# Weighing of values split by queries into two halves, one behind each maximum block

## The chip, the core and the metric

One Trainium2 chip, one of its cores. The metric is the device time of one execution in microseconds (us), as the median of several runs. Everything is one program on one core: TensorE (PE in the profile), VectorE (DVE), ScalarE (ACT), GpSimd (POOL) and the queue of SyncE (SP), each with its own list of instructions, ordered against each other by semaphores.

## What is computed

A block of three layers over x of shape (2, 1024, 128) in float32: half a mixture-of-experts feed-forward, self-attention, half the same feed-forward again. The change touches the attention alone:

```python
qkv = x @ W_qkv_v.T @ W_qkv_u.T            # 16 heads of 8
scores = einsum('bhtd,bhsd->bhts', q, k) / sqrt(8)
attn = softmax(scores)                     # over 1024 keys
y = einsum('bhts,bhsd->bhtd', attn, v)
```

## The kernel before

Attention is cut into 16 **units** (`UNITS`): four heads (`GH`) by 512 queries (`QW`). A unit has eight **chunks** (`CHUNKS`) of 128 keys. A softmax needs the maximum over all keys of a query first, so a unit has two kinds of scores:

- **Maximum blocks** (16 for a unit, `MBLOCKS`): `max_scores(j, part)`, line 1170, writes scores of 128 queries by 512 keys; two parts fill the two banks of `pair[j % 2]`. VectorE's `row_max(j)`, line 914, then takes the maximum of the 1024 columns. With two pairs of banks, TensorE may write block j once block j - 2 is read (`smax_read`). The maxima go through GpSimd (lines 501 to 505), a transpose on TensorE (`m_transpose`, line 1205), a copy on ScalarE (`m_out`, line 659) and a DMA into three more rows of the stack `q_stack`, so that later scores come with the maximum already subtracted. The blocks run ahead: beside chunk c of unit u stand blocks `16(u + 1) + 8 + 2c` and the next one (`blocks_beside`). From chunk 4 of unit 14 on there are none left.
- **Scores of a chunk** (four, one for each head): `scores(u, c, k)`, line 1182, 128 keys by 512 queries, into a ring of three banks (4, 5, 7). ScalarE takes the exponential of each (line 674) into `prob`. The k-th score of the ring can start when ScalarE has read the bank three users back. The transposes of `m_transpose` and `o_transpose` take a turn in the same ring (`bank_users`).

Both kinds use only half of the array's rows: heads 0 and 1 lie in partitions 0 to 63 of the stacks, heads 2 and 3 in 64 to 127. `HEAD_OF_STEP` makes steps 0 and 1 of a chunk heads 2 and 3 (upper half), steps 2 and 3 heads 0 and 1 (lower half). The first block beside a chunk is of a head in the lower half, the second of one in the upper half. Two matmuls on different halves run at the same time.

- **Weighing**: `weigh(u, c)`, line 1191, four float32 matmuls, one for each head, with the values (128 keys by 32 columns) as weights and the exponentials (128 by 512) streamed. The four heads take the four groups of 32 columns of the array and run side by side, in two passes each. They add up over the chunks in bank 6. The weighing waits for all four exponentials of its chunk (`prob_ready`), and the first one of a unit for the copy of bank 6 (`sums_out`, line 691, `oT_ready`). At the end it gives `pv_done`, on which ScalarE waits before it overwrites `prob` two chunks later.

TensorE's order within chunk c, by hand: first block part 0, score 0, first block part 1, score 1, score 2, weighing of chunk c - 1, transposes if any, second block part 0, score 3, second block part 1. In units 14 and 15 some chunks end with work for what follows attention (`beside`: transposes at lines 1216 and 977, projections at line 1225). In chunk 2 TensorE transposes the sums of the unit before (`o_transpose`, line 1199) and VectorE divides by the softmax's denominators (`store_norm`, lines 921 and 924), there between the two maxima of the chunk.

Of the kernel before, what the change touches and what calls it, by code (L numbers as in the profile page):

```python
# [35 lines left out]
GH = 4  # L36
GROUPS = 2 * HEADS // GH
UNITS = 2 * GROUPS
CHUNKS = SEQ // P
QW = 512  # L40
STEPS = CHUNKS * GH
AHEAD = 8
# [28 lines left out]
def bank_users():  # L71

    users = [("m", 0)]
    for u in range(UNITS):
        for c in range(CHUNKS):
            users += [("score", STEPS * u + GH * c + k) for k in range(GH - 1)]
            if c == O_CHUNK and u:
                users.append(("o", u - 1))
            if c == M_CHUNK and u + 1 < UNITS:
                users.append(("m", u + 1))  # L80
            users.append(("score", STEPS * u + GH * c + GH - 1))
    return users + [("o", UNITS - 1)]
# [25 lines left out]
def at_least(eng, sem, value):  # L108

    if not isinstance(value, int) or value > 0:  # L110
        eng.wait_ge(sem, value)


def build(nc, x_in, w_qkv_v, w_qkv_ut, w_o_v, w_o_ut, gate_w, sh_gate, sh_up, sh_down, r_gate, r_up, r_down, out):
# [3 lines left out]
    with ExitStack() as ctx:  # L118
# [426 lines left out]
        def _(act):  # L545
# [64 lines left out]
            def attention():  # L610
# [55 lines left out]
                def unit(u):  # L666

                    turns_left = UNITS - u
                    for c in range(CHUNKS):
                        for k in range(GH):  # L670
# [4 lines left out]
                                                 scale=SCALE).then_inc(prob_ready, 1)  # L675
                            if i == 2 and u:
                                sums_out(u - 1)
                            if i == GH * M_CHUNK + 2 and turns_left > 1:
                                m_out(u + 1)
# [29 lines left out]
        def _(dve):  # L709
# [181 lines left out]
            def attention():  # L891
# [35 lines left out]
                def unit(u):  # L927

                    for c in range(CHUNKS):
                        blocks = blocks_beside(u, c)  # L930
                        for j in blocks[0:1]:
                            row_max(j)
                        if c == O_CHUNK and 0 < u < UNITS - 1:
                            store_norm(u - 1)
                        for j in blocks[1:2]:
                            row_max(j)

# [28 lines left out]
        def _(pe):  # L966
# [146 lines left out]
            def attention():  # L1113
# [70 lines left out]

                def weigh(u, c):

                    pe.wait_ge(prob_ready, STEPS * u + GH * (c + 1))
                    if c == 0:
                        at_least(pe, oT_ready, u)
                    for h in range(GH):  # L1190
                        ins = nc.tensor.matmul(bank[6][32 * h:32 * (h + 1), :], v_grp[u // 2 % 2][:, c, h, :], prob[c % 2 * GH + h],  # L1191
                                               start=(c == 0), stop=(c == CHUNKS - 1))
                    ins.then_inc(pv_done, 1)

# [44 lines left out]
                def unit(u):  # L1239
# [5 lines left out]
                    for c in range(CHUNKS):  # L1245
                        blocks = blocks_beside(u, c)
                        for part in range(2):
                            for j in blocks[0:1]:
                                max_scores(j, part)
                            scores(u, c, part)  # L1250
                        scores(u, c, 2)
                        if c:
                            weigh(u, c - 1)
                        elif u:
                            weigh(u - 1, CHUNKS - 1)
                        if c == O_CHUNK and u:
                            o_transpose(u - 1)
                        if c == M_CHUNK and u + 1 < UNITS:
                            m_transpose(u + 1)
                        for j in blocks[1:2]:  # L1260
                            max_scores(j, 0)
                        scores(u, c, 3)
                        for j in blocks[1:2]:
                            max_scores(j, 1)
                        for work, quad_done in beside.get((UNITS - u, c), ()):
# [14 lines left out]
                for u in range(UNITS):  # L1280
                    unit(u)
                weigh(UNITS - 1, CHUNKS - 1)
                logits(1, 0)
# [35 lines left out]
```

## Time and profile before

| | |
|---|---|
| median of 3 runs | 673.07 us (672.56 to 674.61) |
| the profiled execution | 678.38 us, its span 676.6 us |
| feed-forward, then projections and the stacks | 0 to about 179 us of the span |
| maxima of unit 0 and half of unit 1 | about 180 to 210 us |
| units 0 to 15 | about 210 to 540 us |
| second feed-forward | about 540 to 676.6 us |
| TensorE, VectorE, ScalarE, GpSimd busy | 573.9, 454.8, 376.0, 144.0 us |

The times in the rows are microseconds from the start of the span. A row of the timeline joins neighbouring instructions of the same kind and gives the start of the first, the time until the last one ends, and how many there are. A matmul's duration holds its way through the array, so consecutive ones overlap; what one costs in a row of them is the distance from start to start.

### The profile page before, as it was taken

To read this page: it belongs to the slowest core of one execution; us is meant where nothing else is said; L and a number is where in the kernel's file an instruction comes from. 1 tells how busy PE (TensorE), PEld (TensorE's weight loads), DVE (VectorE), ACT (ScalarE), POOL (GpSimd) and SP (SyncE) were. 2 spreads that over 40 slices of the span, in tenths; PEclk is the share of its full clock that TensorE was granted. 3 is DMA by queue.
4 is the path that set the end of the run, shared out by engine and by line. 5 is a ranking of instruction groups with operands and counts; after the bars stand their busy time and mean duration, and the time that the engine had idled before them with its cause. 6 is when DMAs were issued, how large, how long until landed. Compare 5 with 4: busy or idle time off the path is not lost.

```text
span 676.6 us, 11663 instructions
## 1 busy us (share of the span) xinstructions
PE 573.9 (85%) x3560; PEld 206.0 (30%) x3560; DVE 454.8 (67%) x815; ACT 376.0 (56%) x816; POOL 144.0 (21%) x228
## 2 busy tenths in 40 slices
PE   2984999824589999999999999999999968589991
PEld 2643445412121122222222222222223444434440
DVE  6542334347378999999999999999992557124442
ACT  2211344313404988888988888888888821023340
POOL 2471245513500000000000000000000004414442
PEclk9988999957755999999999999999999969879996
DMA  9995223123321000101000010000000000111114
GB/s 231 325 342 161 82 83 85 44 64 108 141 77 48 2 2 3 47 1 43 8 15 35 1 49 2 2 1 3 1 2 2 1 0 29 46 31 56 50 40 134
DMA packets 52295, 40.56 MB, mean 60 GB/s; under 512 B 4905, under 2 KB 49598, under 8 KB 52240
## 3 DMA queue, kind: packets, MB, share of 16 engines
q1 hardware_dynamic: 49168, 35.58, 17.8%
q0 software_dynamic: 3072, 4.28, 2.0%
q8 instruction: 30, 0.49, 0.3%
q14 instruction: 25, 0.20, 0.1%
HBM read 26.85 MB, written 14.88 MB: 62 GB/s over the span
## 4 chain that ended last, share of the span: by engine, by line
PE 53%; DVE 16%; issue 10%; DMA 8%; ACT 6%; SPq 2%; another core or an unknown queue 2%; POOL 2%; POOLq 0%; DVEq 0%; ACTq 0%
PE bank L1191 13%; PE pair L1170 12%; DVE rowmax L914 9%; PE pair L1061 7%; PE bank L1182 5%; PE bank L1078 4%; ACT arena L674 4%; DMA xe<-rows 3%; PE pair L1070 3%; PE pair L985 2%; POOL rows L467 1%; PE bank L1049 1%; PE bank L1199 1%; PE pair L977 1%
## 5 line engine op out<-in xcount | busy, mean ns | idle before, releaser
L914 DVE TENSOR_REDUCE rowmax<-pair 128x1 f32<-128x1024 f32 x256 | 301.7, 1219 | 29.2 <-PE pair L1170 24.4
L674 ACT ACTIVATE arena<-bank 128x512 f32<-128x512 f32 x512 | 271.5, 605 | 48.9 <-PE bank L1182 43.6
L1182 PE MATMUL bank<-q_stack,k_stack 51*128 51x512 bf16 x512 | 164.9, 388 | 4.1 <-ACT arena L674 1.2
L1170 PE MATMUL pair<-k_stack,q_stack 48*128 48x512 bf16 x512 | 153.6, 407 | 15.0 <-DMA k_stack<-k_parts 5.2
L1191 PE MATMUL bank<-arena 128*32 128x512 f32 x1024 | 137.5, 609 | 0.2 <-ACT arena L674 0.2
L474 POOL DMA_INDIRECT y<-yb,slot_token x64 | 62.9, 982 | 100.0 <-ACT yb L587 82.3
L864 DVE TENSOR_TENSOR arena<-pair,arena 128x256 f32<-128x256 f32 x64 | 27.2, 424 | 82.2 <-ACT arena L582 65.4
L1170 PEld LDWEIGHTS pair<-k_stack,q_stack 48*128 48x128 bf16 x512 | 29.6, 95 | 155.4 <-DVE rowmax L914 130.8
L1061 PE MATMUL pair<-w_exp,xeT 128*64 x128 | 69.1, 623 | 0.4 <-ACT xeT L577 0.4
L1063 PE MATMUL pair<-w_exp,xeT 128*64 128x512 f32 x128 | 69.2, 623 | 0.0
L1182 PEld LDWEIGHTS bank<-q_stack,k_stack 51*128 51x128 bf16 x512 | 39.2, 94 | 66.8 <-ACT arena L674 56.2
L501 POOL TENSOR_TENSOR mpart<-zeros,rowmax 128x16 bf16<-128x16 f32 x16 | 3.5, 222 | 248.1 <-DVE rowmax L914 248.1
L587 ACT ACTIVATE yb<-bank 128x128 f32<-128x128 f32 x64 | 17.8, 277 | 54.1 <-PE bank L1080 48.3
L467 POOL DMA_INDIRECT rows<-xn,slot_i x32 | 31.2, 974 | 74.0 <-DVE slot_i L836 65.1
L977 PE MATMUL pair<-identf,xn 128*128 128x128 f32 x48 | 11.3, 392 | 40.7 <-DVE xn L746 40.3
L1078 PE MATMUL bank<-w_exp,arena 128*64 x256 | 41.6, 285 | 0.2
L1080 PE MATMUL bank<-w_exp,arena 128*64 128x128 f32 x256 | 41.6, 286 | 0.0
L582 ACT ACTIVATE arena<-pair 128x256 f32<-128x256 f32 x64 | 24.6, 385 | 28.3 <-PE pair L1063 27.4
L1015 PE MATMUL bank<-w_sh,arena 128*128 128x128 f32 x128 | 19.0, 311 | 13.9 <-DVE xres L806 12.4
L1191 PEld LDWEIGHTS bank<-arena 128*32 128x32 f32 x1024 | 20.2, 108 | 32.0 <-issue 30.9
L1078 PEld LDWEIGHTS bank<-w_exp,arena 128*64 128x64 f32 x256 | 26.2, 136 | 9.9 <-issue 6.1
L1070 PE MATMUL pair<-identf,arena 128*128 128x128 f32 x128 | 28.0, 300 | 0.0
(135 smaller groups left out, 534.2 us busy)
## 6 DMA issues: line engine op xcount, KB each, us to landing
xe<-rows SPq DMA_DIRECT2D x64, 66.0 KB
w_exp<-in_r_gate SPq DMA_DIRECT2D x4, 1024.0 KB
w_exp<-in_r_up SPq DMA_DIRECT2D x4, 1024.0 KB
w_exp<-in_r_down SPq DMA_DIRECT2D x8, 512.0 KB
rows<-empty_row SPq DMA_DIRECT2D x1, 2112.0 KB, 11.6
rows<-empty_row SPq DMA_DIRECT2D x32, 66.0 KB
xnT<-y SPq DMA_DIRECT2D x8, 256.0 KB, 3.5
q_parts<-arena SPq DMA_DIRECT2D x12, 128.0 KB, 2.6
```

The source lines that it names most:

```text
L467: nc.gpsimd.indirect_dma_start(rows_dram[n], bass.IndirectOffsetOnAxis(slot_i[:, t:t + 1].bitcast(U32), 0), xn[:, t, :], None).then_inc(sc ...
L474: nc.gpsimd.indirect_dma_start(y_dram[n], bass.IndirectOffsetOnAxis(slot_token[:, r:r + 1].bitcast(U32), 0), yb[r % 4][:, :], None, bounds ...
L674: nc.scalar.activation(prob[c % 2 * GH + HEAD_OF_STEP[k]], ring_bank("score", STEPS * u + i), ACT.Exp, scale=SCALE).then_inc(prob_ready, 1)
L914: nc.vector.tensor_reduce(rowmax[u % 2][:, m:m + 1], pair[j % 2][:, :], AX_X, ALU.max).then_inc(smax_read, 1)
L1061: nc.tensor.matmul(bank[r % 2][0:PAGE, :], xeT[r % 2][:, 0:PAGE], w_exp[:, bass.ds(e, 2 * INNER)], start=True, stop=True)
L1063: nc.tensor.matmul(bank[r % 2][PAGE:P, :], xeT[r % 2][:, PAGE:P], w_exp[:, j * WROW:j * WROW + 2 * INNER], start=True, stop=True).then_inc ...
L1070: ins = nc.tensor.transpose(bank[2 + r % 2][:, c * P:(c + 1) * P], h_sb[r % 2][:, c * P:(c + 1) * P], identf[:, :])
L1078: nc.tensor.matmul(bank[(4, 7)[r % 2]][0:PAGE, 0:P], hT_sb[r % 2][:, c * P:c * P + PAGE], w_exp[:, bass.ds(e + at, P)], start=(c == 0), st ...
L1080: ins = nc.tensor.matmul(bank[(4, 7)[r % 2]][PAGE:P, 0:P], hT_sb[r % 2][:, c * P + PAGE:(c + 1) * P], w_exp[:, j * WROW + at:j * WROW + at ...
L1170: ins = nc.tensor.matmul(pair[j % 2][:, part * BANK:(part + 1) * BANK], q_stack[r][rows, half, l, t * P:(t + 1) * P], k_stack[r][rows, l, ...
L1182: nc.tensor.matmul(ring_bank("score", i), k_stack[r][rows, l, c * P:(c + 1) * P], q_stack[r][rows, half, l, :], start=True, stop=True).the ...
L1191: ins = nc.tensor.matmul(bank[6][32 * h:32 * (h + 1), :], v_grp[u // 2 % 2][:, c, h, :], prob[c % 2 * GH + h], start=(c == 0), stop=(c == ...
```

## The change

The weighing is cut by queries into two halves of 256 columns (`PARTS`, `WEIGHED`): `weigh(u, c, w)`. TensorE's order in a chunk becomes: first block part 0, score 0, first block part 1, score 1, weighing's first half, second block part 0, score 2, second block part 1, score 3, weighing's second half, then transposes and the work beside. In chunk 1 both halves stand at the end, since bank 6 is still being copied out. VectorE takes both maxima of a chunk before it divides (`store_norm`). ScalarE's `sums_out` and `m_out` move behind the fourth exponential of their chunk, and the ring's turns for the transposes behind the fourth score. Scores, blocks, exponentials and their number stay.

```diff
+PARTS = 2
+WEIGHED = QW // PARTS
@@ bank_users
-            users += [("score", STEPS * u + GH * c + k) for k in range(GH - 1)]
+            users += [("score", STEPS * u + GH * c + k) for k in range(GH)]
             if c == O_CHUNK and u:
                 users.append(("o", u - 1))
             if c == M_CHUNK and u + 1 < UNITS:
                 users.append(("m", u + 1))
-            users.append(("score", STEPS * u + GH * c + GH - 1))
@@ ScalarE, unit
-                            if i == 2 and u:
+                            if i == 3 and u:
                                 sums_out(u - 1)
-                            if i == GH * M_CHUNK + 2 and turns_left > 1:
+                            if i == GH * M_CHUNK + 3 and turns_left > 1:
                                 m_out(u + 1)
@@ VectorE, unit
-                        for j in blocks[0:1]:
+                        for j in blocks:
                             row_max(j)
                         if c == O_CHUNK and 0 < u < UNITS - 1:
                             store_norm(u - 1)
-                        for j in blocks[1:2]:
-                            row_max(j)
@@ TensorE, weigh
-                def weigh(u, c):
+                def weigh(u, c, w):
 
-                    pe.wait_ge(prob_ready, STEPS * u + GH * (c + 1))
-                    if c == 0:
-                        at_least(pe, oT_ready, u)
+                    cols = slice(w * WEIGHED, (w + 1) * WEIGHED)
+                    if w == 0:
+                        pe.wait_ge(prob_ready, STEPS * u + GH * (c + 1))
+                        if c == 0:
+                            at_least(pe, oT_ready, u)
                     for h in range(GH):
-                        ins = nc.tensor.matmul(bank[6][32 * h:32 * (h + 1), :], v_grp[u // 2 % 2][:, c, h, :], prob[c % 2 * GH + h],
-                                               start=(c == 0), stop=(c == CHUNKS - 1))
-                    ins.then_inc(pv_done, 1)
+                        ins = nc.tensor.matmul(bank[6][32 * h:32 * (h + 1), cols], v_grp[u // 2 % 2][:, c, h, :],
+                                               prob[c % 2 * GH + h][:, cols], start=(c == 0 and w == 0),
+                                               stop=(c == CHUNKS - 1 and w == PARTS - 1))
+                    if w == PARTS - 1:
+                        ins.then_inc(pv_done, 1)
@@ TensorE, unit
-                        for part in range(2):
-                            for j in blocks[0:1]:
-                                max_scores(j, part)
-                            scores(u, c, part)
-                        scores(u, c, 2)
-                        if c:
-                            weigh(u, c - 1)
-                        elif u:
-                            weigh(u - 1, CHUNKS - 1)
+                        weighed = (u, c - 1) if c else (u - 1, CHUNKS - 1)
+                        for w in range(PARTS):
+                            for part in range(2):
+                                for j in blocks[w:w + 1]:
+                                    max_scores(j, part)
+                                scores(u, c, 2 * w + part)
+                            if c != 1 and weighed[0] >= 0:
+                                weigh(*weighed, w)
+                        if c == 1:
+                            for w in range(PARTS):
+                                weigh(*weighed, w)
                         if c == O_CHUNK and u:
                             o_transpose(u - 1)
                         if c == M_CHUNK and u + 1 < UNITS:
                             m_transpose(u + 1)
-                        for j in blocks[1:2]:
-                            max_scores(j, 0)
-                        scores(u, c, 3)
-                        for j in blocks[1:2]:
-                            max_scores(j, 1)
@@ TensorE, after the units
-                weigh(UNITS - 1, CHUNKS - 1)
+                for w in range(PARTS):
+                    weigh(UNITS - 1, CHUNKS - 1, w)
```

## Rows read from the trace of the kernel before

**Rows 1.** The page's first part: busy time, share of the span, instructions.
```profile
PE 573.9 (85%) x3560; PEld 206.0 (30%) x3560; DVE 454.8 (67%) x815; ACT 376.0 (56%) x816; POOL 144.0 (21%) x228
```

**Rows 2.** Groups of instructions, 240 to 500: busy us, mean ns; idle us before, by releaser.
```profile
L914 DVE TENSOR_REDUCE rowmax<-pair 128x1 f32<-128x1024 f32 x206 | 242.6, 1219 | 10.1 <-PE pair L1170 5.8
L674 ACT ACTIVATE arena<-bank 128x512 f32<-128x512 f32 x412 | 218.5, 605 | 33.9 <-PE bank L1182 29.0
```

**Rows 3.** Waits, 240 to 500: who for whom, total us, times, longest us.
```profile
PEld pair L1170 <- DVE rowmax L914: 96.9, 148, 0.8
```

**Rows 4.** Timeline of VectorE: start, us until last end; ends of 13 units, then one.
```profile
240.23 7.16 DVE L914 TENSOR_REDUCE rowmax<-pair 128x1 f32<-128x1024 f32 x6
...
358.89 2.36 DVE L914 TENSOR_REDUCE rowmax<-pair 128x1 f32<-128x1024 f32 x2 [0.26 <-PE pair L1170]
...
361.87 7.16 DVE L914 TENSOR_REDUCE rowmax<-pair 128x1 f32<-128x1024 f32 x6
...
503.76 3.62 DVE L914 TENSOR_REDUCE rowmax<-pair 128x1 f32<-128x1024 f32 x3
```

**Rows 5.** The same timeline asked for stretches that hold two neighbouring maxima each.
```profile
352.53 2.48 DVE L914 TENSOR_REDUCE rowmax<-pair 128x1 f32<-128x1024 f32 x2
353.80 2.35 DVE L914 TENSOR_REDUCE rowmax<-pair 128x1 f32<-128x1024 f32 x2
354.94 2.56 DVE L914 TENSOR_REDUCE rowmax<-pair 128x1 f32<-128x1024 f32 x2
```

**Rows 6.** Timeline of TensorE in short stretches, one chunk of unit 7.
```profile
353.16 0.39 PE L1182 MATMUL bank<-q_stack,k_stack 51*128 51x512 bf16 x1
...
353.89 0.37 PE L1170 MATMUL pair<-k_stack,q_stack 48*128 48x512 bf16 x1
354.11 0.37 PE L1170 MATMUL pair<-k_stack,q_stack 48*128 48x512 bf16 x1
354.32 0.38 PE L1182 MATMUL bank<-q_stack,k_stack 51*128 51x512 bf16 x1
354.63 0.64 PE L1191 MATMUL bank<-arena 128*32 128x512 f32 x4
355.08 0.61 PE L1191 MATMUL bank<-arena 128*32 128x512 f32 x4
355.63 0.39 PE L1170 MATMUL pair<-k_stack,q_stack 48*128 48x512 bf16 x1
```

**Rows 7.** Timeline, the weight loads (PEld) of that weighing.
```profile
354.63 0.16 PEld L1191 LDWEIGHTS bank<-arena 128*32 128x32 f32 x8 [0.30 <-issue]
```

**Rows 8.** Timeline of ScalarE: after the score of 353.16, and four exponentials on end.
```profile
353.59 2.31 ACT L674 ACTIVATE arena<-bank 128x512 f32<-128x512 f32 x4 [0.17 <-PE bank L1182]
...
522.40 2.06 ACT L674 ACTIVATE arena<-bank 128x512 f32<-128x512 f32 x4 [0.32 <-PE bank L1182]
```

**Rows 9.** Timeline of TensorE: transposes of the sums, the block behind them.
```profile
340.33 0.65 PE L1199 MATMUL bank<-identf,oT 128*128 128x128 f32 x4
...
340.92 0.39 PE L1170 MATMUL pair<-k_stack,q_stack 48*128 48x512 bf16 x1
```

**Rows 10.** Timeline of VectorE in chunks 1 and 2 of unit 0.
```profile
217.25 2.35 DVE L914 TENSOR_REDUCE rowmax<-pair 128x1 f32<-128x1024 f32 x2 [2.03 <-PE pair L1170]
219.91 7.23 DVE L914 TENSOR_REDUCE rowmax<-pair 128x1 f32<-128x1024 f32 x6 [0.30 <-PE pair L1170]
```

**Rows 11.** The stretch 216 to 218: busy us of the engines, TensorE's granted clock.
```profile
216.00:218.00 2.00, 2.00 (x12) 0.53 (x8) 0.75 (x1) 0.92 (x2) 0.00 (x0) 0.50 0.12 49
```

**Rows 12.** Timeline of TensorE in unit 15, where no blocks are left.
```profile
520.98 1.07 PE L1191 MATMUL bank<-arena 128*32 128x512 f32 x8
...
523.05 0.39 PE L1182 MATMUL bank<-q_stack,k_stack 51*128 51x512 bf16 x1 [0.47 <-ACT arena L674]
...
531.72 1.07 PE L1191 MATMUL bank<-arena 128*32 128x512 f32 x8
...
534.15 1.06 PE L1191 MATMUL bank<-arena 128*32 128x512 f32 x8
```

## The prediction

> **What bounds the kernel now.** I read the page first: TensorE is busy for 85% of the span, VectorE for 67%, ScalarE for 56% [rows 1]. That mixes stages, so the groups of instructions for 240 to 500 us come next, the stretch of whole attention units. There VectorE's maxima alone are busy for 242.6 of 260 us and ScalarE's exponentials for 218.5 [rows 2]; and in the waits TensorE stands 96.9 us waiting for a maximum to free its banks, in 148 places [rows 3]. It looks as if VectorE were the bound, with 10.1 us of idle time left to win [rows 2]. That reading is too coarse, and the timeline of VectorE shows why. One unit takes (503.76 - 240.23) / 13 = 20.27 us [rows 4]. Neighbouring maxima start at 352.53, 353.80 and 354.94 us [rows 5]: the steps are 1.27, 1.14 and, since the pair from 354.94 lasts 2.56 us against 1.22 us for one, 1.34 us. A maximum is shown busy for 1.22 us but can follow the one before by 1.14, because the two overlap; so a step of 1.27 is a wait of 0.13 that no idle column shows. Every second step is short (1.14: the data had been there), every other one is 1.26 to 1.48 and more at chunk 2. VectorE's floor for a chunk is 2 x 1.142 = 2.284 us; the chunks take 2.40 to 2.56.
>
> What it waits for is a **loop through TensorE**, read from one chunk [rows 6]. The maximum that starts at 352.53 ends at 353.75 and frees its pair; 0.11 us later (353.86, a plain release elsewhere takes 0.05) come first block part 0 (353.89), part 1 with score 1 beside it (354.11), score 2 (354.32), the weighing (354.63), second block part 0 (355.63) and, 0.22 later, part 1 (355.85), whose result is there 0.38 us later; the next maximum of that pair of banks starts at 356.27. From the end of a maximum to there it is 2.46 to 2.52 us, in which nothing waits but for a little at score 2 (its bank). The second block is late because the whole weighing, 1.00 us, stands ahead of it. Two maxima end to end (1.142 + 1.214 = 2.356) and this path (2.46) make two chunks: (2.356 + 2.46) / 2 = 2.41 us for one, which is what is seen. Whatever else stands in that path (o_transpose 0.59 us [rows 9], m_transpose, one matmul, so at most a step of 0.22, score 2 waiting behind the copy of the sums) is added in full: hence gaps like the 0.26 us [rows 4]. So neither TensorE's throughput nor VectorE's bounds it, but the order between them.
>
> **The change, part by part.**
>
> *TensorE's own work for a chunk.* Start to start [rows 6]: block to block with a score beside it 0.22; last score to weighing 0.31; first to second pass of the weighing 0.45; second pass to the next block 0.55. Before: four such steps of 0.22 (parts of both blocks; scores 0, 1, 3 ride beside them), 0.31 and 1.00: 2.19 us. After: each half of a chunk has 0.226 + 0.306 and half a weighing. A pass streams 512 columns in 0.427 (0.45 less what the first loads cost, 0.026); with half the columns it is 0.213, so a half weighing takes 0.24 + 0.33 = 0.57, and half a chunk 0.226 + 0.306 + 0.57 = 1.10, the chunk 2.20. The cut costs 0.14 of streaming overhead and one more change of shape (0.09), and wins the 0.22 in which score 2 had no block beside it: nothing in sum. The eight weight loads of a weighing now meet passes half as long; they are through in 0.16 us [rows 7], which is under 0.213, so I cost them at nothing; uncovered they would be 0.16 for each half (below). Bound of the half weighing from both sides: 0.50 (exactly half) and 1.00 (no shorter at all); I take 0.57, since the pass's length follows the columns in the transposes too: four of 128 float32 columns take 0.65 us in all [rows 9].
>
> A rule of the Trainium skill speaks against the change here: TensorEngine Tiling (Array Packing), Tiling Modes, says that changing the tiling mode drains the engine. The row agrees in kind: 0.31 instead of 0.22 into the weighing, and about 0.1 out of it, 0.2 for a round trip. With two round trips instead of one the page's rule makes the chunk 0.2 us longer on TensorE, and that is in the 2.20 above.
>
> *The path to the blocks.* A release, 0.05 to 0.12; part 0, part 1 0.226; result and start of the maximum 0.41: 0.70 to 0.76 us after the maximum of that pair has ended. The other pair's maximum gives 1.142 - 0.07 = 1.07 us of cover. So VectorE finds every block ready as long as TensorE comes less than 0.3 to 0.37 us after the release; by its own work (1.10 for half a chunk against VectorE's 1.142) it comes 0.04 early. VectorE becomes the bound: 2.284 us for a chunk.
>
> *Where a wait is new.* The first half now stands behind score 1 and waits for all exponentials of the chunk before; behind it on TensorE are second block and scores 2 and 3, on which VectorE and ScalarE wait. Score to exponential 0.43 (353.16 to 353.59), exponentials on end (2.06 - 0.60) / 3 = 0.48 apart [rows 8]. From the start of score 2: exponential 2 at 0.43, exponential 3 at 0.90, its end 1.50, seen at 1.56; TensorE is there at 1.142 + 0.53 = 1.67. It fits by 0.11. The turns of the ring's three banks have more room. ScalarE's load is 4 x 0.48 = 1.93 for a chunk: below the bound.
>
> *Chunks with extra work.* Chunk 1 has no half weighing in the middle and both at its end, four passes on end, about 1.00: its next block is 0.39 after its release, against 0.37 of cover: 0.02 lost. Chunk 2: transposes 0.59 [rows 9] at its end; VectorE divides after both maxima, 0.62 us from the end of a maximum to the next (361.25 to 361.87 [rows 4]). The transposes are through about 0.2 before VectorE asks for them, and the division gives TensorE the time for them. Score 2 of chunk 3 waits for the division (ring) about when it comes up anyway. m_transpose, under 0.22, goes into the cover. The copy of the sums moves one exponential later; the weighings that wait for it are at chunk 1's end. The moved DMA of m (its issue follows ScalarE's copy) has three chunks to land. So a unit is 16 x 1.142 + 0.62 + 0.02 = 18.9 us, by TensorE's own count 8 x 2.20 + 0.59 + 0.2 - 0.2 = 18.2, hidden. **Gain 20.27 - 18.9 = 1.35 a unit**, for the 13 units of [rows 4] and the one from 219.91 to 240.23: 14 x 1.35 = -18.9 us.
>
> *Beginning.* In unit 0 the clock is at 0.50 (1.2 GHz) until about 218 [rows 11], and VectorE idles 2.03 and 0.30 us behind a cold weighing of 1.9 us [rows 10]. With second block ahead of it the idle comes in two smaller pieces; I get the maximum of 219.91 at about 219.1: -0.8, and +0.5 at worst if the clock rises later.
>
> *End.* Without blocks (from chunk 4 of unit 14) the cut only costs: the scores 1 and 2 and the scores 3 and 0 no longer stand next to each other on different halves. A plain chunk is 2.39 now (weighing at 520.98; last score before the next at 523.05, plus 0.31) with 0.47 of waiting for ScalarE [rows 12]; after, TensorE alone needs 2 x (0.215 + 0.317 + 0.57) = 2.20: -0.2, in four chunks. A chunk with transposes beside it is 2.43 (531.72 to 534.15 [rows 12]), no waiting; after 2.20 + 0.59 = 2.79: +0.35, in about seven with such work, projections too. In sum +1.6.
>
> Sum: -18.9 - 0.8 + 1.6 = -18.1. The profiled execution (678.38, span 676.6) becomes 660.3; the runs' median stands 5.3 under the profiled one, so 673.07 - 18.1 = **655.0 us**.
>
> **Rivals.**
>
> 1. *TensorE becomes the bound.* If a half weighing costs 0.65 instead of 0.57, a chunk is 2.36 and a unit 8 x 2.36 + 0.55 = 19.4: -0.85 x 14 = -12, -0.8, +2.5 at the end: 663. It decides from 0.61. Against: the count above has few unknown terms; for: all its margin is 0.04 in 1.14.
> 2. *ScalarE's exponentials hold the first half.* The margin is 0.11; behind the copy of the sums or a late score they may slip, and each 0.1 beyond it in every chunk costs 8 x 14 x 0.1 = 11 us: 662 with 0.17 too little. The loop score 3, exponential, half weighing, score 2, score 3 is 2.13, shorter than 2.284, so it should recover.
> 3. *Slower: the weight loads come out of their cover.* If each half shows its loads (0.16), half a chunk is 1.26, a chunk 2.53, a unit 20.8: +0.5 x 14 = +7, the end 12 x 0.32 + 1.6 = +5: 685. It beats the gain from 0.11 a half on. Against: today the loads of the second pass run during the first [rows 7]. The Trainium skill, TensorE: Matmul & The Clock Gate, Part 3, says that LDWEIGHTS overlaps matmuls in flight only where the row groups differ, and all of these use all rows; by that rule this rival would hold. The row of eight loads in 0.16 us under two passes of 0.45 goes against it.
> 4. *No change*: VectorE can't go on at 1.142. Only every second step shows it, always after a wait. If on end it were 1.20, a unit would be 19.8 and the sum -6; at 1.23 nothing is left.
>
> **How the numbers follow.** Forecast, VectorE bound in the units, 651 to 659: 0.66. Rivals 1 and 2 and the mild form of 4, 659 to 671: 0.20. Within 0.3% (about what a measurement of this kernel tells from no change): 0.04. Rival 3: 0.08. Better than 651: 0.02. For 8 in 10 the range goes from 651.3 to 663. Faster 0.88, same 0.04, slower 0.08.
>
> **What the profile will show.** Right: steps between maxima of 1.14 throughout, idle only at chunk 2; a unit of 18.9; TensorE's waits on the maxima short and before each of both blocks; pass to pass 0.24 in the weighing. Rival 1: TensorE without waits, VectorE idle by PE at each block. Rival 2: weighing released by ScalarE. Rival 3: loads standing between passes. The prediction would be wrong above all by a half weighing over 0.61 us or a floor of the maxima over 1.15.

## The result and the profile after

| | before | after |
|---|---|---|
| median | 672.85 us (672.56 to 674.61, 4 runs) | 656.47 us (656.3 to 658.39, 4 runs) |
| ratio | 1 | 0.9768 (95% interval 0.9752 to 0.9784) |
| span of the profiled execution | 676.6 us | 656.6 us |
| one attention unit | 20.27 us | 19.09 us |

The change makes the kernel 2.3% faster: 15.6 us by the ratio (14.5 to 16.7 by its interval). 18.1 us (655.0) had been forecast. The page of the changed kernel, first part, as [rows 1] of before:

```profile
PE 557.6 (85%) x4584; PEld 214.0 (33%) x4584; DVE 447.0 (68%) x815; ACT 380.8 (58%) x816; POOL 144.1 (22%) x228
```

TensorE has 1024 matmul records more (each float32 matmul leaves two) and is busy for less time. The two spans differ by more (20.0 us) than the runs do. The rest lies in the second feed-forward: from the end of the last reciprocal of the attention to the end of the span the profiled execution of before took 134.7 us, the thirteen other profiles of this study, with the same feed-forward, 129.1 to 130.1. The chain of work of before shows where. It holds two waits that no other of these profiles has in its chain, cut_alone included, whose feed-forward is within 0.6 us of it until then; the profile does not name what ended them:

```profile
574.42 10.01 another core or an unknown queue
584.48 2.80 another core or an unknown queue
```

So the account goes by stages of the attention, on VectorE's timeline. The kernel after, one unit (start, us until the last end), for [rows 4]:

```profile
336.03 16.00 DVE L915 TENSOR_REDUCE rowmax<-pair 128x1 f32<-128x1024 f32 x14
352.33 2.36 DVE L915 TENSOR_REDUCE rowmax<-pair 128x1 f32<-128x1024 f32 x2 [0.29 <-PE pair L1169]
354.60 0.25 DVE L922 RECIPROCAL rden<-bank 128x16 f32<-128x16 f32 x1
...
355.13 16.00 DVE L915 TENSOR_REDUCE rowmax<-pair 128x1 f32<-128x1024 f32 x14
```

Fourteen maxima run on without a visible gap, (16.00 - 1.22) / 13 = 1.137 us apart; before they stood in groups of six, eight and two. One gap is left, 0.29 us, ahead of chunk 2. The unit is 355.13 - 336.03 = 19.10 us, 19.09 on average. Stretches that hold two neighbouring maxima, for [rows 5]:

```profile
326.08 2.35 DVE L915 TENSOR_REDUCE rowmax<-pair 128x1 f32<-128x1024 f32 x2
327.21 2.34 DVE L915 TENSOR_REDUCE rowmax<-pair 128x1 f32<-128x1024 f32 x2
```

The step is 1.13 us, at every place but three in a unit; before, every other one was 1.26 or more. TensorE, half a chunk in short stretches, for [rows 6]:

```profile
336.73 0.38 PE L1169 MATMUL pair<-k_stack,q_stack 48*128 48x512 bf16 x1
337.04 0.42 PE L1192 MATMUL bank<-arena 128*32 128x256 f32 x4
337.28 0.40 PE L1192 MATMUL bank<-arena 128*32 128x256 f32 x4
337.61 0.39 PE L1169 MATMUL pair<-k_stack,q_stack 48*128 48x512 bf16 x1
```

Score to half weighing 0.31, first to second pass 0.24, second pass to the next block 0.33: the half weighing is 0.57 us, as forecast, and half a chunk 1.107 us (forecast 1.10). The waits for the maxima in 240 to 490 us, for [rows 3] (10 us less of window), and the new one for the exponentials:

```profile
PEld pair L1169 <- DVE rowmax L915: 56.1, 124, 0.8
PEld bank L1192 <- ACT arena L675: 27.6, 65, 0.4
```

These figures, like those of [rows 3], are idle time of the weight loads (PEld) and not of TensorE's matmuls, so they are no measure of what TensorE loses. The weighing's matmuls themselves show 0.0 us of idle time in 240 to 480 us, and both halves start 0.31 us after the score ahead of them, the one that waits for exponentials and the one that does not.

The last division of the attention starts at 541.68 before and at 527.32 after:

```profile
541.68 0.26 DVE L921 RECIPROCAL rden<-bank 128x16 f32<-128x16 f32 x1 [4.85 <-PE bank L1199]
```

```profile
527.32 0.26 DVE L922 RECIPROCAL rden<-bank 128x16 f32<-128x16 f32 x1 [5.56 <-PE bank L1202]
```

Counted from the first maximum of all (179.73 and 180.55) that is 361.95 and 346.77 us, 15.2 us less: -0.4 up to chunk 3 of unit 0 (forecast -0.8), -16.6 in the fourteen units from there to chunk 3 of unit 14 (forecast -18.9), +1.8 from there to the division (forecast +1.6). That lies within the interval of the runs' gain.

### The profile page after: what moved, and what is told of

Its sections match the earlier page's. It is cut to its first block, busy times and chain, and to the rows that moved or that the text cites. A ratio compares the mean times of both kernels' runs of the same rounds, so it can differ in the third digit from the quotient of the medians.

```text
span 656.6 us, 13711 instructions
## 1 busy us (share of the span) xinstructions
PE 557.6 (85%) x4584; PEld 214.0 (33%) x4584; DVE 447.0 (68%) x815; ACT 380.8 (58%) x816; POOL 144.1 (22%) x228
## 4 chain that ended last, share of the span: by engine, by line
PE 56%; DVE 22%; DMA 9%; issue 6%; POOL 4%; SPq 2%; ACT 1%; POOLq 0%; DVEq 0%; ACTq 0%
PE bank L1192 15%; DVE rowmax L915 15%; PE pair L1169 13%; PE pair L1060 8%; PE bank L1077 5%; DMA xe<-rows 4%; POOL rows L468 3%; PE pair L1069 3%; PE bank L1181 3%; PE pair L984 2%; PE bank L1202 1%; PE bank L1048 1%; PE pair L976 1%; DMA rows<-xn,slot_i 1%; DMA xnT<-y 1%
## 5 line engine op out<-in xcount | busy, mean ns | idle before, releaser
L915 DVE TENSOR_REDUCE rowmax<-pair 128x1 f32<-128x1024 f32 x256 | 294.8, 1216 | 21.6 <-PE pair L1169 21.6
L675 ACT ACTIVATE arena<-bank 128x512 f32<-128x512 f32 x512 | 276.5, 600 | 31.2 <-PE bank L1181 25.7
L1169 PE MATMUL pair<-k_stack,q_stack 48*128 48x512 bf16 x512 | 164.5, 408 | 14.9 <-DVE rowmax L915 8.9
L1192 PE MATMUL bank<-arena 128*32 128x256 f32 x2048 | 161.4, 393 | 0.2 <-ACT arena L675 0.2
L1181 PE MATMUL bank<-q_stack,k_stack 51*128 51x512 bf16 x512 | 159.7, 386 | 0.5 <-ACT arena L675 0.5
L1192 PEld LDWEIGHTS bank<-arena 128*32 128x32 f32 x2048 | 42.2, 108 | 99.3 <-issue 63.7
L1181 PEld LDWEIGHTS bank<-q_stack,k_stack 51*128 51x128 bf16 x512 | 30.7, 94 | 17.1 <-ACT arena L675 15.6
L1048 PE MATMUL bank<-identf,xe 128*128 128x128 f32 x64 | 19.8, 310 | 17.9 <-DMA xe<-rows 17.8
L578 ACT ACTIVATE xeT<-bank 128x128 f32<-128x128 f32 x64 | 17.5, 273 | 26.7 <-PE bank L1048 26.2
```

Of the source, the lines that this page charges most:

```text
L675: nc.scalar.activation(prob[c % 2 * GH + HEAD_OF_STEP[k]], ring_bank("score", STEPS * u + i), ACT.Exp, scale=SCALE).then_inc(prob_ready, 1)
L915: nc.vector.tensor_reduce(rowmax[u % 2][:, m:m + 1], pair[j % 2][:, :], AX_X, ALU.max).then_inc(smax_read, 1)
L1169: ins = nc.tensor.matmul(pair[j % 2][:, part * BANK:(part + 1) * BANK], q_stack[r][rows, half, l, t * P:(t + 1) * P], k_stack[r][rows, l, ...
L1181: nc.tensor.matmul(ring_bank("score", i), k_stack[r][rows, l, c * P:(c + 1) * P], q_stack[r][rows, half, l, :], start=True, stop=True).the ...
L1192: ins = nc.tensor.matmul(bank[6][32 * h:32 * (h + 1), cols], v_grp[u // 2 % 2][:, c, h, :], prob[c % 2 * GH + h][:, cols], start=(c == 0 a ...
```

## Experiments

**Is it the cut or the order?** The two parts of the change, each alone. First the cut in the old order (`weigh` with its `cols` as in the change, only its calls shown):

```diff
-                        if c:
-                            weigh(u, c - 1)
-                        elif u:
-                            weigh(u - 1, CHUNKS - 1)
+                        weighed = (u, c - 1) if c else (u - 1, CHUNKS - 1)
+                        for w in range(PARTS):
+                            if weighed[0] >= 0:
+                                weigh(*weighed, w)
```

> The kernel before, its order of instructions untouched, only each weighing cut into two halves of 256 queries that follow each other at once. Theory (the cut itself costs and gives nothing, the order does it): four passes on end, 0.24 + 2 x 0.22 + 0.33 = 1.00 us, as one uncut weighing; unit 20.3 us, time 671 to 675. Rival (the cut makes the weighing cheaper, or its doubled weight loads show): a unit under 20.0, or each weighing 0.1 us longer and the time 5 us or more above that of before.

672.97 us, ratio 1.0007 (0.9993 to 1.0021). The weighing of sixteen records takes what the eight took, 1.01 us until the next block (353.84 is the last score ahead of it), and a unit 20.30 us. The cut costs nothing and gives nothing by itself.

```profile
353.84 0.38 PE L1184 MATMUL bank<-q_stack,k_stack 51*128 51x512 bf16 x1
354.14 1.07 PE L1195 MATMUL bank<-arena 128*32 128x256 f32 x16
355.15 0.39 PE L1172 MATMUL pair<-k_stack,q_stack 48*128 48x512 bf16 x1
```

Then the changed kernel's order with the weighing whole:

```diff
-PARTS = 2
+PARTS = 1
@@ unit
-                        for w in range(PARTS):
+                        for i in range(2):
                             for part in range(2):
-                                for j in blocks[w:w + 1]:
+                                for j in blocks[i:i + 1]:
                                     max_scores(j, part)
-                                scores(u, c, 2 * w + part)
-                            if c != 1 and weighed[0] >= 0:
-                                weigh(*weighed, w)
+                                scores(u, c, 2 * i + part)
+                            if i == 0 and c != 1 and weighed[0] >= 0:
+                                weigh(*weighed, 0)
                         if c == 1:
-                            for w in range(PARTS):
-                                weigh(*weighed, w)
+                            weigh(*weighed, 0)
```

> The changed kernel's order, but the weighing whole, ahead of the second block (in chunk 1 at the end, as there). Theory (the serial path from the end of a maximum to the second block sets the pace): the path is 0.05 to 0.12 + 0.23 + 0.31 + 1.00 + 0.23 + 0.41 = 2.23 to 2.30 us, without score 2's 0.22, so a chunk is (1.13 + 1.21 + 2.26) / 2 = 2.30 us against 2.26 with halves; a unit 19.2 to 19.5, the time 656 to 662. Rival (only the halves free the second block): a chunk stays at 2.40 or more, the time at 668 to 673.

690.52 us, ratio 1.0271 (1.0249 to 1.0292): slower than before, by 18 us, more than the change gained. Both the theory and the rival were wrong, and so was the prediction's account of the old kernel by a single loop. Its timeline on TensorE and ScalarE, from score 3 (the row of 340.06) on:

```profile
340.06 0.38 PE L1181 MATMUL bank<-q_stack,k_stack 51*128 51x512 bf16 x1
340.26 2.06 ACT L675 ACTIVATE arena<-bank 128x512 f32<-128x512 f32 x4 [0.50 <-PE bank L1181]
...
341.40 0.16 PEld L1192 LDWEIGHTS bank<-arena 128*32 128x32 f32 x8 [0.40 <-ACT arena L675]
...
342.40 0.39 PE L1181 MATMUL bank<-q_stack,k_stack 51*128 51x512 bf16 x1
...
342.63 0.38 PE L1181 MATMUL bank<-q_stack,k_stack 51*128 51x512 bf16 x1
```

Score 3 starts at 340.06; exponential 2 occupies ScalarE from 340.26, exponential 3 follows 0.48 later and lasts 0.60; the weighing waits for it until 341.40; scores 2 and 3 stand behind the whole weighing, at 342.40 and 342.63. That is a loop through ScalarE of 2.57 us, and VectorE's maxima come in the same beat: steps of 1.14 and 1.43, a unit of 21.45 us.

**The whole weighing behind everything.** If that loop is the cause, the weighing should be harmless where its exponentials are long done (edit against order_alone):

```diff
-                            if i == 0 and c != 1 and weighed[0] >= 0:
-                                weigh(*weighed, 0)
-                        if c == 1:
+                        if weighed[0] >= 0:
                             weigh(*weighed, 0)
```

> As order_alone, but the whole weighing always at the end of the chunk, behind both blocks and all four scores. New theory (order_alone is paced by a loop through ScalarE: score 3, two exponentials, whole weighing, scores 2 and 3 of the next chunk, 0.69 + 0.60 + 0.05 + 1.00 + 0.23 = 2.57 us): at the end the weighing finds its exponentials done, so only the path of the maxima is left, (1.13 + 1.21 + 2.26) / 2 = 2.30 us a chunk; a unit 19.1 to 19.6 us, 656 to 662. Rival (a whole weighing ahead of any block holds VectorE up beyond that path, by contention or cover): a unit over 20.5, time over 672.

673.09 us, ratio 1.0007 (0.9997 to 1.0016); a unit of 20.12 us. Neither holds in full: the time is the rival's, the unit is neither's. (The time is no shorter than before although the unit is, because the stretch from chunk 3 of unit 14 to the last division takes 40.5 us instead of 36.8.) A chunk is 2.40 us and not 2.30, and the timeline shows another loop, through the ring of banks:

```profile
341.69 0.39 PE L1181 MATMUL bank<-q_stack,k_stack 51*128 51x512 bf16 x1
...
342.12 2.06 ACT L675 ACTIVATE arena<-bank 128x512 f32<-128x512 f32 x4 [0.33 <-PE bank L1181]
...
342.76 0.09 PEld L1181 LDWEIGHTS bank<-q_stack,k_stack 51*128 51x128 bf16 x1 [0.32 <-ACT arena L675]
...
343.08 1.06 PE L1192 MATMUL bank<-arena 128*32 128x512 f32 x8
344.08 0.39 PE L1181 MATMUL bank<-q_stack,k_stack 51*128 51x512 bf16 x1
```

Score 0 at 341.69, its exponential 0.43 later, 0.60 long; score 3 takes the same bank, so it starts 0.05 after that, at 342.77; then 0.31 into the weighing and 1.00 until the next score 0: 2.39 us. In the kernel before, the same sum goes round from score 3 over score 2 (which takes its bank) to the whole weighing and the next score 3. It had been in view: a chunk without any block was 2.39 us, with a wait for ScalarE [rows 12].

**Two loops in the kernel before.** That gives a new theory: two loops of nearly the same length, VectorE's 2.41 us and ScalarE's 2.39. Shortening either alone should give little, both together much.

```diff
-                    nc.vector.tensor_reduce(rowmax[u % 2][:, m:m + 1], pair[j % 2][:, :], AX_X, ALU.max).then_inc(smax_read, 1)
+                    nc.vector.tensor_reduce(rowmax[u % 2][:, m:m + 1], pair[j % 2][:, 0:BANK], AX_X, ALU.max).then_inc(smax_read, 1)
```

> The kernel before, with maxima over 512 of each block's 1024 columns (half the keys left out of the subtracted maximum): a maximum goes from 1.14 to 0.60 us in step and from 1.21 to 0.68 in length. Theory (two loops of nearly the same length held the old chunk: VectorE's path at 2.41 us, and one through ScalarE and the ring of three banks, score 3 to exponential 0.43, exponential 0.60, release 0.05, score 2 to weighing 0.31, whole weighing 1.00 = 2.39 us): the first falls to 1.87, the second stays, so a chunk is 2.39 to 2.40 and a unit still over 19.9 us instead of 20.27. Rival (the path of the maxima alone, as the prediction had it): a chunk of 2.19, TensorE's own work, a unit under 18.7 us.

664.43 us, ratio 0.9882 (0.9856 to 0.9908); a unit of 20.13 us, 0.14 less than before. Most of the gain of the run comes ahead of chunk 3 of unit 0: 7.1 us, of which 5.9 in the first 24 maxima. VectorE in the units, for [rows 4]:

```profile
296.09 1.29 DVE L914 TENSOR_REDUCE rowmax<-pair 128x1 f32<-128x512 f32 x2 [1.11 <-PE pair L1170]
298.49 1.29 DVE L914 TENSOR_REDUCE rowmax<-pair 128x1 f32<-128x512 f32 x2 [1.11 <-PE pair L1170]
```

With maxima half as long the chunk is still 298.49 - 296.09 = 2.40 us; the time shows as idle. The other side:

```diff
-                            nc.scalar.activation(prob[c % 2 * GH + HEAD_OF_STEP[k]], ring_bank("score", STEPS * u + i), ACT.Exp,
+                            nc.scalar.activation(prob[c % 2 * GH + HEAD_OF_STEP[k]][:, 0:QW // 2], ring_bank("score", STEPS * u + i)[:, 0:QW // 2], ACT.Exp,
                                                  scale=SCALE).then_inc(prob_ready, 1)
```

> The kernel before, with exponentials over 256 of the 512 queries (half of the exponentials left out): 0.21 us less for each. Theory of two loops: ScalarE's loop falls to 2.18, VectorE's stays at 2.41 but loses what score 2 waited for in it, so a unit falls by 0.1 to 0.6 us from 20.27. Rival (ScalarE's loop alone): a chunk of 2.19, a unit under 18.7 us.

665.50 us, ratio 0.9898 (0.9868 to 0.9927); a unit of 19.90 us, 0.37 less. And both edits (half of the keys left out of the maximum, half of the exponentials left out):

> Both cuts at once on the kernel before. Theory of two loops: only now does the chunk fall to TensorE's own 2.19 us, a unit of 18.3 to 18.8 us, much more than the two single gains together. Rival (one loop): no more than the larger of the single gains.

636.75 us, ratio 0.9483 (0.9462 to 0.9503); a unit of 18.42 us. 0.14 and 0.37 alone, 1.85 together: neither loop alone held the kernel. All three runs came out as the theory of two loops had said. The chunk is TensorE's own 2.19 us now, as counted in the prediction (296.46 - 294.27):

```profile
294.27 1.29 DVE L914 TENSOR_REDUCE rowmax<-pair 128x1 f32<-128x512 f32 x2 [0.90 <-PE pair L1170]
296.46 1.29 DVE L914 TENSOR_REDUCE rowmax<-pair 128x1 f32<-128x512 f32 x2 [0.90 <-PE pair L1170]
```

**ScalarE's part in the slow order.** The same shortening of the exponentials on order_alone:

> order_alone with exponentials over 256 of the 512 queries (half of them left out). Theory (order_alone was paced by the loop score 3, exponential 3, whole weighing, score 2, score 3, 2.57 us): it falls to 0.43 + 0.39 + 0.05 + 1.00 + 0.23 = 2.10, so VectorE's path, 2.30 us, sets the pace: a unit of 19.0 to 19.6 us instead of 21.45. Rival (the whole weighing ahead of the second block is what cost it, whatever ScalarE does): a unit over 20.5 us.

661.06 us, ratio 0.9833 (0.9808 to 0.9858); a unit of 19.47 us instead of 21.45:

```profile
298.10 0.25 DVE L922 RECIPROCAL rden<-bank 128x16 f32<-128x16 f32 x1
...
317.57 0.25 DVE L922 RECIPROCAL rden<-bank 128x16 f32<-128x16 f32 x1
```

With ScalarE's loop short, the whole weighing ahead of the second block costs what the path of the maxima said it would. The same short exponentials in the old order gave 19.90 us (before_half_exp): with ScalarE's loops out of the way, the order alone is worth 0.43 us of a unit. With full exponentials it costs 1.18 us, and only the halves turn that into a gain, because ScalarE's loops then go round with 0.57 us of weighing in them instead of 1.00.

**Do the weight loads stay hidden?** Each half cut once more, two quarters of 128 queries behind each block (i = 0, 1 now counts the blocks):

```diff
-PARTS = 2
+PARTS = 4
@@ unit
                             if c != 1 and weighed[0] >= 0:
-                                weigh(*weighed, w)
+                                for w in (2 * i, 2 * i + 1):
+                                    weigh(*weighed, w)
```

> The changed kernel with the weighing in four quarters of 128 queries, two behind each block, so that each pass is 0.107 us and stands before its own weight loads (0.106 us each, four at a time). Theory (a pass can't be shorter than its loads, but loads do run beside the pass before): 0.13 us a pass, two quarters 0.64 us, half a chunk 1.18 us on TensorE, which then sets the pace: a unit near 20.0, time 666 to 671. Rival A (loads cost nothing even here): 656 to 657. Rival B (each pass waits for its loads in full, 0.24 us): a unit near 23, over 700.

659.23 us, ratio 0.9790 (0.9772 to 0.9809); a unit of 19.17 us, 0.08 more than with halves. The theory's 0.64 us for two quarters was wrong, rival A nearly right: the loads cost next to nothing even here, 0.005 us in half a chunk. Four passes on end, TensorE at 346.03 and the next block at 346.60:

```profile
346.03 0.64 PE L1192 MATMUL bank<-arena 128*32 128x128 f32 x16
346.60 0.39 PE L1169 MATMUL pair<-k_stack,q_stack 48*128 48x512 bf16 x1
```

The sixteen records are two quarters with two passes of four heads each; 0.57 us to the next block is the half weighing's time to a hundredth. Passes follow each other by 0.109 us, with four loads of 0.11 us each beside every one.

**What bounds the changed kernel?** Maxima over 896 of a block's 1024 columns (the ends of the two lines):

```diff
-pair[j % 2][:, :], AX_X, ALU.max)
+pair[j % 2][:, 0:896], AX_X, ALU.max)
```

> The changed kernel with maxima over 896 of each block's 1024 columns: VectorE's step can fall from 1.13 to 1.00 us (this leaves out an eighth of the keys from the subtracted maximum). Theory (TensorE's count, 1.107 for half a chunk, is just behind VectorE's 1.131): a unit is 8 x 2.21 + 0.59 + 0.16 + 0.55 (chunk 1) = 19.0 us against 19.09, 654.5 to 656.5. Rival (VectorE alone bounds it): 16 x 0.13 = 2.1 us less a unit, 627.

655.17 us, ratio 0.9738 (0.9723 to 0.9753), as the theory had said; the trace has 1.5 us less in the first 24 maxima. The unit stays at 19.09 us to the second decimal:

```profile
331.78 0.26 DVE L922 RECIPROCAL rden<-bank 128x16 f32<-128x16 f32 x1
```

```profile
348.61 2.20 DVE L915 TENSOR_REDUCE rowmax<-pair 128x1 f32<-128x896 f32 x2 [0.68 <-PE pair L1169]
350.88 0.26 DVE L922 RECIPROCAL rden<-bank 128x16 f32<-128x16 f32 x1
```

350.88 - 331.78 = 19.10. What VectorE saves comes back as idle time, 0.68 instead of 0.29 ahead of chunk 2, and most steps are 1.11, TensorE's half chunk. From block to block on TensorE every chunk of the unit takes the same time in both kernels, to 0.001 us. The changed kernel is paced by TensorE's list, with what it waits for in chunk 1, and not by VectorE. Chunk 1 of a unit of the changed kernel, on TensorE, ScalarE and VectorE, shows what makes its chain so long:

```profile
329.83 0.39 PE L1181 MATMUL bank<-q_stack,k_stack 51*128 51x512 bf16 x1
...
330.12 0.60 ACT L692 ACTIVATE oT<-bank 128x512 f32<-128x512 f32 x1
330.60 2.09 ACT L675 ACTIVATE arena<-bank 128x512 f32<-128x512 f32 x4
330.74 0.39 PE L1169 MATMUL pair<-k_stack,q_stack 48*128 48x512 bf16 x1 [0.30 <-DVE rowmax L915]
...
331.27 0.39 PE L1181 MATMUL bank<-q_stack,k_stack 51*128 51x512 bf16 x1
331.59 1.07 PE L1192 MATMUL bank<-arena 128*32 128x256 f32 x16
332.60 0.39 PE L1181 MATMUL bank<-q_stack,k_stack 51*128 51x512 bf16 x1
...
333.23 1.22 DVE L915 TENSOR_REDUCE rowmax<-pair 128x1 f32<-128x1024 f32 x1 [0.29 <-PE pair L1169]
```

Score 0 starts at 329.83. Its exponential, due at 330.26, starts at 330.60, behind the copy of the sums; score 3 needs that bank and starts at 331.27 instead of 330.96; behind it both halves; the next chunk at 332.60. Chunk 1 is 2.77 us, the other seven 2.21 but for extra work: 7 x 2.213 + 2.77 + 0.59 + 0.16 (the transposes) + 0.08 (a score waiting for m's copy) = 19.09.

TensorE stands twice in this chunk: 0.46 us for a maximum (330.74 instead of 330.28), then 0.31 us at score 3. The first wait does not set the chunk's length. In shorter_max, where the maxima are done earlier, the same chunk (from 345.20) reads:

```profile
345.43 0.38 PE L1169 MATMUL pair<-k_stack,q_stack 48*128 48x512 bf16 x1
...
345.88 0.39 PE L1169 MATMUL pair<-k_stack,q_stack 48*128 48x512 bf16 x1
...
346.65 0.39 PE L1181 MATMUL bank<-q_stack,k_stack 51*128 51x512 bf16 x1 [0.16 <-ACT arena L675]
...
347.97 0.39 PE L1169 MATMUL pair<-k_stack,q_stack 48*128 48x512 bf16 x1
```

Now the block waits 0.23 us and score 3 waits 0.54: 0.77 again, and 2.77 us for the chunk. What fixes it is one chain through ScalarE: score 0, copy of the sums 0.29 later, exponential 0.48 later, score 3 0.67 later, 0.32 into both halves, 1.01 to the next chunk.

**The copy one exponential later** takes it from between score 0 and its exponential:

```diff
-                            if i == 3 and u:
+                            if i == 4 and u:
                                 sums_out(u - 1)
```

> The changed kernel, with ScalarE's copy of the sums one exponential later (behind the first of chunk 1). Theory: VectorE's extra 0.37 us before the first maximum of chunk 2 comes from score 3 of chunk 1, which waits 0.31 us for the first exponential, which waits for the copy. With the copy behind it score 3 is on time, the double weighing waits 0.1 us for the copy instead: 0.2 us less in each of 14 units, 653.0 to 654.5. Rival (the double weighing at the end of chunk 1 alone makes it): no change, within 0.5 us.

654.82 us, ratio 0.9745 (0.9727 to 0.9764). The unit is 18.99 us, 0.10 less and not 0.2: score 3 is on time, but the double weighing then waits for the copy, 0.5 us behind score 3 instead of 0.31. In direction as expected, half the size, and the time just above the forecast range; against the changed kernel the intervals overlap, so the gain is shown by the trace and not by the runs.

**The old order where there are no blocks** (`weigh` ahead of score 3; what follows `else:` is as before, indented):

```diff
+                        if not blocks:
+                            for k in range(3):
+                                scores(u, c, k)
+                            for w in range(PARTS):
+                                weigh(*weighed, w)
+                            scores(u, c, 3)
+                        else:
```

> The changed kernel, with the old order (scores 0, 1, 2, both halves at once, score 3) in the twelve chunks that have no blocks. Theory: there the new order costs TensorE 0.25 us more for a chunk, which shows in the chunks with transposes or projections beside them: 1.5 to 2 us less, 654.5 to 655.2, units with blocks unchanged at 19.09 us. Rival (the end is bound by ScalarE or by the chain of projections): within 0.5 us of the changed kernel.

654.71 us, ratio 0.9744 (0.9728 to 0.9760). Units with blocks are 19.09 us as in the changed kernel, the stretch behind them is 1.54 us shorter than there, as the theory had said. Here too the interval overlaps that of the changed kernel. A chunk of unit 15 with transposes beside it, first in the changed kernel (from score to score), then here (from weighing to weighing):

```profile
518.91 0.60 PE L1181 MATMUL bank<-q_stack,k_stack 51*128 51x512 bf16 x2
...
521.70 0.60 PE L1181 MATMUL bank<-q_stack,k_stack 51*128 51x512 bf16 x2
```

```profile
513.36 1.07 PE L1192 MATMUL bank<-arena 128*32 128x256 f32 x16
...
515.80 1.07 PE L1192 MATMUL bank<-arena 128*32 128x256 f32 x16
```

2.79 and 2.44 us; 2.79 and 2.43 were the prediction's numbers for after and before.

**Both of these:**

> copy_later and tail_order together on the changed kernel. Theory (two separate places, the units with blocks and the chunks without): the gains add, 0.11 us in each of 14 units and 1.7 us at the end, 652.9 to 653.8. Rival (they hide one another): 654.3 or more.

655.94 us, ratio 0.9742 (0.9728 to 0.9755). The gains did not add, as the rival had it. From the first maximum to the start of the last division the trace has 344.8 us, against 346.8 in the changed kernel, 345.1 with the copy alone and 344.8 with the end alone. By stages, against the changed kernel: the units keep the copy's gain (18.99 us, -1.4 in fourteen), the end is 0.56 us shorter and not 1.54, and the beginning is the same, where both single edits had been 0.5 us shorter.

The end is a collision of the two edits. In chunk 1 of unit 15 the weighing waits for the copy of the sums. The late copy pushes it back by 0.27 us where it stands behind all scores (copy_later), but by 0.98 us where the old order puts it behind score 2. It starts 16.20 us after unit 14's first maximum of chunk 3 (486.33) in tail_order and 17.18 us after it (487.17) in both:

```profile
502.53 1.07 PE L1192 MATMUL bank<-arena 128*32 128x256 f32 x16
```

```profile
504.35 1.07 PE L1192 MATMUL bank<-arena 128*32 128x256 f32 x16 [1.05 <-ACT oT L692]
```

The beginning goes with the granted clock, which rises from 0.50 to 1.00 in unit 0. In the changed kernel and in both it rose 39.2 and 39.3 us after the first maximum, with the two edits alone 38.0 and 38.1 us, and the beginning took 41.0 us in the former and 40.5 in the latter. In unit 0 all four run the same instructions, so this part is no gain of the edits. No version here is better than either single edit by more than the runs can tell.

## Why the prediction was right, and where it was not

- **Size and direction**: right. The range (651.3 to 663.0) holds 656.47, and the forecast was 1.5 us off. In part this was luck: the unit came out 0.17 us from the forecast, although what bounds it was named wrongly (below).
- **What bounds the kernel before**: half right. Reading the starts instead of the idle column gave the hidden waits of every second maximum, and VectorE's path of 2.41 us is real. But "nothing waits but for a little at score 2 (its bank)" passed over a second loop, through ScalarE and the ring, of 2.39 us. before_half_max, before_half_exp and before_half_both show it: 0.14, 0.37 and 1.85 us of a unit. The row that should have led there was used for the end only [rows 12]. The forecast did not suffer from it, because the unit of before was taken from the rows and only the loops of the changed kernel were reckoned. The prediction also read [rows 3] as time in which TensorE stands; it is idle time of its weight loads.
- **TensorE's work**: right. The half weighing is 0.57 us, half a chunk 1.107 (1.10 forecast), so the chunk is 2.21 us against the 2.19 that before_half_both shows for the old order: 0.02 for "nothing in sum".
- **The wait of the first half on ScalarE**: right by the loop with halves (2.13 us, under a chunk). The same sum with a whole weighing, 2.57, was not made; it would have told that the cut is necessary and not only the order (order_alone, then order_half_exp).
- **"VectorE becomes the bound"**: the step that failed. TensorE's own count for a unit was put at 18.2 us and called hidden; its list takes 19.09, and VectorE's maxima wait for it (shorter_max). Missing are 0.77 us in chunk 1, taken as 2.0: the copy of the sums delays the exponential of score 0, that delays the bank of score 3, and both halves stand behind score 3. The prediction had said of this copy only that the weighings waiting for it "are at chunk 1's end". The rest is 0.007 for each half chunk and 0.08 at m's copy. Chunk 1's loss was forecast at 0.02 us for VectorE; it is 0.37 (a step of 1.50 instead of 1.13). How the 2.77 us would fall without the copy is only in part known: copy_later wins 0.10 of them.
- **VectorE's floor**: 1.142 was taken, 1.131 is what it does on end, 0.18 us a unit less; the division costs 0.53 us and not 0.62. These two errors partly made up for chunk 1 and the small losses. So a unit came out at 19.09 for 18.92, and the units' gain at 16.6 for 18.9.
- **Beginning and end**: -0.4 for -0.8. The clock rose 0.4 us later than in the profile of before, counted from the first maximum (39.2 against 38.8); where it rose at 38.0 (copy_later) the beginning came out at the forecast -0.8. The end is +1.8 for +1.6, a chunk with transposes 2.79 us as counted.
- **Rivals**: 1 (TensorE as the bound) held in kind, through chunk 1 and not through a dearer half. Of 2, an exponential behind the copy of the sums did hold TensorE up, but at score 3 and not at the first half. 3 (weight loads) fell: quarters shows next to none of it. The rule of TensorE: Matmul & The Clock Gate, Part 3 (the Trainium skill), that LDWEIGHTS overlaps only matmuls of other row groups, does not agree with these rows; all loads here use all rows, and they hide beside passes that follow each other by 0.109 us (quarters). 4 (no change) fell: fourteen maxima at 1.137.

What stays open: why the clock rises up to 1.5 us earlier or later in one profile than in another, and how short chunk 1 could be with the copy of the sums out of its chain altogether.

## What to carry to other kernels

Follow every cycle that goes through a limited set of buffers, not only the one that ends at the busiest engine, and add up each: here two loops of 2.41 and 2.39 us hid each other, and the experiments that shortened one alone looked as if neither mattered. A long instruction group that stands in several loops can be worth cutting even if the cut saves no work, because each loop then holds only a part of it. And a special case once in eight chunks can hold as much as the regular ones leave: count the chain of the whole period, irregular chunks included.

## What was not expected of the hardware

- A maximum over 1024 columns is recorded at 1.21 to 1.23 us but follows the one before by 1.13 us (after). Waits under 0.08 us, and the first 0.08 us of longer ones, show in no idle column: the step of 1.50 us ahead of chunk 2 is 0.37 over 1.13 and shows as 0.29.
- Four float32 passes of 128 columns with their own weight loads (0.11 us each, four at a time) take 0.57 us to the next matmul, as two passes of 256 do: hardly any cost of a shorter pass was seen down to one pass every 0.109 us (quarters).
